# Who copies the transposed queries and keys, and where the first norm transposes stand

## The chip, the cores and the metric

The kernel runs on one NeuronCore of a Trainium2 chip. Its engines work side by side and meet only at semaphores: TensorE (PE in the profile; its weight loads are listed apart as PEld), VectorE (DVE), ScalarE (ACT), GpSimd (POOL) and SyncE (SP), which issues most of the transfers. The metric is the device time of one execution in microseconds, as the median of several runs; lower is better.

## The reference, cut to what matters

There are 16 images of 192 channels and 32 x 32 pixels (1024 tokens). Each passes three layers:

```python
# layer 0: channel attention on a convolved projection
xn = (x - mu) * rsqrt(var + eps) * ln_g + ln_b           # over a whole image
Q, K, V = proj(xn)            # per head of 24 channels: 24 x 24 product, then 3 x 3 depthwise convolution
attn = softmax(einsum("bhnc,bhnd->bhcd", K, Q) / alpha)  # 24 x 24 for each of 8 heads, summed over tokens
x = einsum(V, attn), then w_f, + b_f + xn
# layer 1: causal attention over the 1024 tokens, 6 heads of 32
t = t + attention(ln(t), W_qkv) @ W_proj @ W_proj + ...
# layer 2: 4 experts, each token goes to its best two
t = t + sum over 2 chosen experts of gate * (gelu(ln(t) @ w1 + b1) @ w2 + b2)
```

Layers 0 and 1 are computed image by image. The experts run after the last image, in 67 blocks of 512 rows.

## The kernel before, in words

Each engine has its own program, written out by hand; nothing reorders it. An engine takes its instructions in the written order, and waits stand in it as `wait_ge(semaphore, count)`. What matters here is the part of one image `i` in three stages.

**Stage 1, convolution and channel attention.** PE runs six rounds `conv(i, r)`: four of them ("pair" rounds, p = 0 to 3) give queries and keys of two heads each, two give values. Every round is 32 recorded matmuls of 32 columns by 512 (L1724). ScalarE takes a round out of PSUM with `conv_out` (L1510). For a pair round PE then transposes eight 128 x 128 pieces, `conv_transposes` (L1738): four into PSUM bank 4, four into bank 5. `conv_qk` copies them to the tensor `qkt`: bank 4 on VectorE (L1027, signals `qkT_sb`), bank 5 on ScalarE (L1514, signals `qkT_sb2`). `channel_products(i, f)` (L1751) multiplies keys by queries of two pairs, so it waits for both signals of pairs 2f and 2f + 1; the transposes of pair p wait for the copies of pair p - 1.

Between these copies VectorE does the routing of image `i - 1`, cut into the steps `route(i - 1, 0)` to `route(i - 1, 6)`: gate logits, second layer norm, which two experts a token takes, and the row of each token in its expert's blocks. Step 1 ends with `rowsum` (L1179), the number of tokens per expert; PE's `counts` (L1920, L1921) waits for it and stands between `channel_products(i, 0)` and `conv(i, 4)`. For image 0 the same places hold the steps of `finish_setup`, which prepare weights.

**Stage 2, the tokens.** PE puts together the image's 8 chunks of 128 tokens, one PSUM bank each (`token_bank(k) = k % 6`): `input_and_first_heads(i, k)` (L1772 to L1778) and `last_heads(i, k)` (L1782). VectorE adds a bias to each chunk (L1089, signals `y_sb`), takes its statistics (L1049 to L1056); GpSimd computes the inverse root (L753); VectorE normalises four chunks at a time, `normed(i, 0)` and `normed(i, 1)` (L1065, signals `xhat_sb`). `norm_transposes(i, 0)` on PE (L1791) waits for the first four normalised chunks, which come from token chunks 0 to 3, and writes banks 6 and 7. Chunk 6 reuses the bank of chunk 0 and chunk 7 that of chunk 1, so they wait for `y_sb`.

Then ScalarE copies the transposed tokens (`high_channels`, L1533), VectorE subtracts that copy to get the low part (`low_channels`, L1073 and L1076), and PE makes queries and keys in six groups of five products, `queries_keys` (L1808): the first two products of the first group read the high part, the third waits for L1073, the fourth for L1076. Values (L1816) stand between the groups.

**Stage 3, the softmax attention** of layer 1: 48 units of scores, maxima, exponentials, transposes and products. Its last units hold rounds 0 and 1 of the next image's convolution.

Of the kernel before, what the change touches and what calls it, by code (L numbers as in the profile page):

```python
# [11 lines left out]
ACT = mybir.ActivationFunctionType  # L12
# [3 lines left out]
P = 128  # L16
# [3 lines left out]
def hybrid_block_kernel(nc, x, ln_g, ln_b, conv_w, conv_bias_row, conv_taps, conv_bias, alpha_rows, w_f_t, b_f,  # L20
# [4 lines left out]
    NC = N // P  # L25
# [20 lines left out]
    TPC = BANK // P  # L46
    PAIRS = NH // 2
# [27 lines left out]
    with ExitStack() as ctx:  # L75
# [3 lines left out]
        def at(name, shape, dt, offset):  # L79
            return nc.alloc_sbuf_tensor_at(name, shape, dt, offset=base + offset)  # L80
# [121 lines left out]
        qkt = at("qkt", [P, NC, PAIRS, P], F32, R)  # L202
# [65 lines left out]
        def bank(b, n=1):  # L268
            return ps[:, b * BANK:(b + n) * BANK]
# [4 lines left out]
        def sems(text):  # L274
            return map(sem, text.split())


        conv_ps, qkT_ps, logit_ps, attnT_ps, mix_ps, y_ps = sems("conv_ps qkT_ps logit_ps attnT_ps mix_ps y_ps")
# [4 lines left out]
        chain, qkT_sb, qkT_sb2, lm_sb, attn_sb, attnT_sb, y_sb, veps, xhat_sb, T_lo, qk_lo, mx_sb, PT_dve, linv_sb, at_sb, o_sb = sems(  # L283
            "chain qkT_sb qkT_sb2 lm_sb attn_sb attnT_sb y_sb veps xhat_sb T_lo qk_lo mx_sb PT_dve linv_sb at_sb o_sb")
# [182 lines left out]
        def token_bank(k):  # L467
            return k % 6
# [437 lines left out]
        def _(dve):  # L906
# [116 lines left out]

            def conv_qk(i, p):

                dve.wait_ge(qkT_ps, 2 * (PAIRS * i + p) + 1)
                v.tensor_copy(qkt[:, 0:TPC, p, :], bank(4).rearrange("p (k c) -> p k c", c=P)).then_inc(qkT_sb, 1)  # L1027

# [469 lines left out]
        def _(act):  # L1498
            a = nc.scalar
# [10 lines left out]
                a.activation(dst, bank(2 * (r % 2), 2), ACT.Identity, bias=convb[:, col:col + 1]).then_inc(conv_sb, 1)  # L1510

            def conv_qk(i, p):
                act.wait_ge(qkT_ps, 2 * (PAIRS * i + p) + 2)
                a.activation(qkt[:, TPC:NC, p, :], bank(5).rearrange("p (k c) -> p k c", c=P), ACT.Copy  # L1514
                             ).then_inc(qkT_sb2, 1)
# [170 lines left out]
        def _(pe):  # L1686
# [20 lines left out]
            def conv(i, r):  # L1707
                kind, n = ROUNDS[r]
                if kind == "pair":
                    pe.wait_ge(ring_ld[n], RING_LOADS * (i + 1))  # L1710
                    tiles = [(2 * n + j % 2, W * (j // 2)) for j in range(4)]
                else:
                    tiles = [(HPH * n + j, 2 * W) for j in range(4)]
                if r >= 2:
                    pe.wait_ge(conv_sb, NR * i + r - 1)
                elif i:

                    pe.wait_ge(exp_sb, NU * (i - 1) + NU - 1 + r)
                for nh in range(QC):
                    for s in range(2):  # L1720
                        for j, (h, c0) in enumerate(tiles):
                            rhs = ring[h // 2][s][0:KROWS[s], h % 2, :].rearrange(
                                "p (a b) -> p a b", b=PW)[:, SH // QC * nh:SH // QC * (nh + 1), 0:SW]
                            last = t.matmul(bank(2 * (r % 2) + nh)[W * j:W * (j + 1), :],  # L1724
                                            wconv[s][0:KROWS[s], h, c0:c0 + W], rhs,
                                            start=s == 0, stop=s == 1, skip_group_check=True)
                last.then_inc(conv_ps, 1)
# [28 lines left out]
            def attention_transpose(i, f):  # L1756
                pe.wait_ge(attn_sb, 2 * i + f + 1)
                t.transpose(bank(6 + f)[0:2 * W, P:2 * P], lm[:, f, :], ident[:, :]).then_inc(attnT_ps, 1)
# [10 lines left out]
            def input_and_first_heads(i, k):  # L1769

                o = bank(token_bank(k))
                t.matmul(o[:, 0:HALF], xn[:, 0, P * k:P * (k + 1)], ident[0:HALF, 0:HALF],  # L1772
                         start=True, stop=False, skip_group_check=True)
                t.matmul(o[:, C:CE], xn[:, 0, P * k:P * (k + 1)], gcol[:, :], start=False, stop=False,
                         skip_group_check=True)
                t.matmul(o[:, HALF:CE], xn[:, 1, P * k:P * (k + 1)], ident_g[:, :], start=False, stop=False,
                         skip_group_check=True)
                t.matmul(o[:, 0:CE], vp[:, 0, P * k:P * (k + 1)], mix[:, 0, :], start=False, stop=False,  # L1778
                         skip_group_check=True)

            def last_heads(i, k):
                t.matmul(bank(token_bank(k))[:, 0:CE], vp[:, 1, P * k:P * (k + 1)], mix[:, 1, :], start=False, stop=True,  # L1782
                         skip_group_check=True).then_inc(y_ps, 1)

            def norm_transposes(i, j):
                pe.wait_ge(xhat_sb, NC * i + TPC * (j + 1))
                for b, c0 in ((NORM_BANK[j], 0), (NORM_BANK[j] + 1, P)):
                    if c0:
                        pe.wait_ge(xtwice_sb, 2 * i + j + 1)
                    for kk in range(TPC):  # L1790
                        last = t.transpose(bank(b)[:, P * kk:P * (kk + 1)],  # L1791
                                           xhat[j][:, kk, c0:c0 + P], ident[:, :])
                    last.then_inc(lnT_ps, 1)
# [133 lines left out]
            for i in range(B):  # L1927
                conv(i, 2)
                conv_transposes(i, 1)
                conv(i, 3)  # L1930
                channel_products(i, 0)
                if i:
                    counts(i - 1)
                conv(i, 4)
                conv_transposes(i, 2)
                attention_transpose(i, 0)
                conv(i, 5)
                mixing(i, 0)
                conv_transposes(i, 3)
                pe.wait_ge(mix_sb, 2 * i + 1)  # L1940
                pe.wait_ge(xn_flat, 2 * (i + 1))
                pe.wait_ge(conv_sb, NR * i + 5)
                input_and_first_heads(i, 0)
                channel_products(i, 1)
                input_and_first_heads(i, 1)
                pe.wait_ge(conv_sb, NR * i + 6)
                input_and_first_heads(i, 2)
                attention_transpose(i, 1)
                input_and_first_heads(i, 3)
                mixing(i, 1)  # L1950
                input_and_first_heads(i, 4)
                pe.wait_ge(mix_sb, 2 * i + 2)
                for k in range(4):
                    last_heads(i, k)
                input_and_first_heads(i, 5)
                for k in range(4, 6):
                    last_heads(i, k)
                for k in (6, 7):
                    pe.wait_ge(y_sb, NC * i + k - 5)
                    input_and_first_heads(i, k)  # L1960
                    last_heads(i, k)
                norm_transposes(i, 0)
                for n in range(QK_FIRST):
                    queries_keys(i, n)
                for k in range(2):
                    values_of_tokens(i, k)
                norm_transposes(i, 1)
                for k in range(2, 4):
                    values_of_tokens(i, k)
                for n in range(QK_FIRST, NQ):  # L1970
                    queries_keys(i, n)
                for k in range(4, NC):
                    values_of_tokens(i, k)
                if not i:
                    pe.wait_ge(setup_pool, 8)
                for n in SCORED_FIRST:
                    query_scores(i, n)
                for n, (qc, h) in enumerate(SOFT):
                    for m in SCORED[n]:
                        query_scores(i, m)  # L1980
                    if n == NU - 1 and i + 1 < B:
                        conv(i + 1, 0)
                    blocks(i, n)
                    if i + 1 < B and n in STAT_UNITS:
                        image_stat(i, STAT_UNITS.index(n))
                    if h == 5:
                        four_heads(i, qc)
                    if qc and h == 1:
                        two_heads(i, qc - 1)
                        norms(i, qc - 1)  # L1990
                    if qc and h == 3:
                        output_projection(i, qc - 1)
                if i + 1 < B:
                    conv(i + 1, 1)
                two_heads(i, NC - 1)
                norms(i, NC - 1)
                if i + 1 < B:
                    conv_transposes(i + 1, 0)
                output_projection(i, NC - 1)
# [158 lines left out]
```

## Time and profile before

| what | value |
|---|---|
| median of 3 runs | 3286.74 us (3281.87 to 3288.63) |
| the profiled execution | 3286.35 us |
| its span, first to last instruction | 3284.4 us |
| mean granted TensorE clock, as a share of full speed | 0.988 |
| one image, start of its first channel products to the next one's (image 4 to 5) | 132.2 us |
| busy share of PE, DVE, ACT, POOL | 93%, 67%, 57%, 27% |

The 16 images take the first 2220 us or so of the span, the experts the rest. The images from 1 on repeat each other to within 0.1 us in stages 1 and 2, so one image stands for them all; image 0 (with the setup) and image 15 are different. Image 6 is the one shown. Times in the rows are microseconds from the start of the span.

### The profile page before, as it was taken

Reading aid. Unit: us, or ns where it says so; the run is one execution under the profiler, and the core shown is the slowest. Engines: PE = TensorE matmul, PEld = TensorE weight load, DVE = VectorE, ACT = ScalarE, POOL = GpSimd, SP = SyncE. Lnnn points to the kernel's source line nnn. Section 1 sums busy time; section 2 is a strip of 40 time slices with the busy share of each in tenths; the row PEclk is TensorE's granted clock in tenths of the full one; section 3 lists DMA queues with packets and bytes.
Section 4 is the critical chain, followed back from the end, with each engine's and each line's share of the span. In section 5 each row is a group of like instructions: output and inputs, shape, how many; then the busy total and the mean of one; then the engine's idle time right before and its main releaser. Section 6 shows DMA issues by size and latency. Waiting matters only on the chain.

```text
span 3284.4 us, 72525 instructions
## 1 busy us (share of the span) xinstructions
PE 3069.6 (93%) x26642; PEld 2351.2 (72%) x26642; DVE 2203.7 (67%) x5632; ACT 1870.8 (57%) x3996; POOL 877.6 (27%) x1142
## 2 busy tenths in 40 slices
PE   4999999999999999999999999989999999999995
PEld 1767667666666676766766667668888888888884
DVE  3777677677776777777767877665565555555553
ACT  0548466475574664745647548465555555555553
POOL 2112303313123032131331322352133233233233
PEclk9999999999999999999999999999999999999997
DMA  7446445464464554644545446345676677677673
GB/s 181 133 117 174 127 119 150 122 159 122 125 167 114 142 139 111 180 116 127 150 117 160 121 120 177 100 140 172 187 228 217 203 217 220 202 218 222 199 217 118
DMA packets 256517, 519.83 MB, mean 158 GB/s; under 512 B 70919, under 2 KB 161991, under 8 KB 246521
## 3 DMA queue, kind: packets, MB, share of 16 engines
q1 hardware_dynamic: 222878, 453.58, 49.3%
q0 software_dynamic: 29184, 59.81, 6.1%
q8 instruction: 217, 3.56, 0.5%
q10 hardware_dynamic: 4107, 1.81, 0.3%
q14 instruction: 131, 1.07, 0.1%
HBM read 242.82 MB, written 117.71 MB: 110 GB/s over the span
## 4 chain that ended last, share of the span: by engine, by line
PE 68%; DVE 13%; issue 10%; ACT 3%; POOL 3%; DMA 2%; SPq 1%; DVEq 0%; ACTq 0%; POOLq 0%
PE ps L2048 14%; PE ps L1859 9%; PE ps L2064 9%; PE ps L1847 5%; PE ps L1724 5%; PE ps L2069 5%; PE ps L1808 3%; PE ps L1881 3%; PE ps L1891 2%; PE ps L2024 2%; PE ps L1816 2%; ACT p_sb L1544 2%; DVE minus_max L1095 1%; PE ps L1899 1%; PE ps L2033 1%
## 5 line engine op out<-in xcount | busy, mean ns | idle before, releaser
L1095 DVE TENSOR_REDUCE minus_max<-ps 128x1 f32<-128x128 f32 (+7 forms) x768 | 571.7, 749 | 225.7 <-PE ps L1849 215.2
L1544 ACT ACTIVATE p_sb<-ps,minus_max 128x128 f32<-128x128 f32 (+7 forms) x768 | 570.2, 743 | 42.3 <-DVE minus_max L1095 38.9
L1859 PE MATMUL ps<-ident,p_sb 128*128 128x128 f32 x3456 | 532.8, 279 | 43.5 <-ACT p_sb L1544 15.3
L1429 DVE TENSOR_TENSOR g_lo<-g,g_hi 128x512 fp32r<-128x512 f32 x402 | 281.6, 701 | 362.4 <-ACT g_hi L1670 362.4
L1669 ACT ACTIVATE g<-ps,bcur 128x512 f32<-128x512 f32 x402 | 277.0, 689 | 432.8 <-PE ps L2048 427.5
L1558 ACT ACTIVATE PT<-ps 128x512 f32<-128x512 f32 (+3 forms) x768 | 397.3, 517 | 134.4 <-PE ps L1859 125.4
L1859 PEld LDWEIGHTS ps<-ident,p_sb 128*128 128x128 f32 x3456 | 371.5, 142 | 98.3 <-issue 35.9
L2064 PE MATMUL ps<-w_all,g_hi 128*128 x1608 | 436.5, 352 | 1.7 <-DVE y_rows L1453 1.6
L1847 PE MATMUL ps<-KS,QS 96*128 96x512 f32 (+3 forms) x1152 | 395.0, 402 | 22.6 <-ACT p_sb L1544 19.5
L1724 PE MATMUL ps<-ring,wconv 125*32 125x512 f32 (+1 forms) x3072 | 357.2, 603 | 15.8 <-DMA ring<-padded_scratch 15.8
L817 POOL DMA_INDIRECT routed_rows<-xhat,slot x256 | 254.6, 995 | 349.1 <-issue 346.5
L878 POOL DMA_INDIRECT got<-expert_rows,slot x256 | 258.4, 1009 | 326.1 <-issue 265.4
L765 POOL COPY inverse_wide<-inverse_sums 128x192 f32<-128x192 f32 x128 | 44.2, 346 | 1023.5 <-DVE inverse_sums L1116 1023.5
L2069 PE MATMUL ps<-w_all,g_lo 128*128 x1608 | 292.2, 263 | 0.3 <-DVE g_lo L1429 0.3
L2069 PEld LDWEIGHTS ps<-w_all,g_lo 128*128 128x128 f32 x1608 | 289.3, 188 | 3.0 <-DVE g_lo L1429 1.2
L2064 PEld LDWEIGHTS ps<-w_all,g_hi 128*128 128x128 f32 x1608 | 263.9, 191 | 26.6 <-DVE y_rows L1453 2.4
L1670 ACT ACTIVATE g_hi<-ps,bcur 128x512 fp32r<-128x512 f32 x402 | 273.7, 681 | 0.0
L2048 PE MATMUL ps<-X_hi,cur 128*128 128x512 f32 x780 | 255.6, 409 | 7.1 <-ACT g_hi L1670 4.9
L1847 PEld LDWEIGHTS ps<-KS,QS 96*128 96x128 f32 x1152 | 197.7, 196 | 71.3 <-ACT p_sb L1544 42.8
L2048 PE MATMUL ps<-X,cur 128*128 128x512 f32 x780 | 244.6, 395 | 0.0
L1724 PEld LDWEIGHTS ps<-ring,wconv 125*32 125x32 f32 (+1 forms) x3072 | 93.3, 110 | 207.5 <-issue 193.9
L1108 DVE COPY PT<-ps 128x128 f32<-128x128 f32 (+3 forms) x384 | 184.4, 480 | 68.4 <-PE ps L1859 68.3
(293 smaller groups left out, 5465.6 us busy)
## 6 DMA issues: line engine op xcount, KB each, us to landing
ring<-padded_scratch SPq DMA_DIRECT2D x576, 204.0 KB
cur<-w_all SPq DMA_DIRECT2D x65, 1536.0 KB, 7.1
routed_rows<-zero_rows SPq DMA_DIRECT2D x67, 384.0 KB, 5.1
xgt<-routed_rows SPq DMA_DIRECT2D x67, 384.0 KB, 4.1
expert_rows<-y_rows SPq DMA_DIRECT2D x67, 384.0 KB, 3.3
padded_scratch<-xpad SPq DMA_DIRECT2D x32, 435.0 KB, 3.6
x_sb<-x SPq DMA_DIRECT2D x16, 768.0 KB, 5.5
KS<-QKh SPq DMA_DIRECT2D x128, 96.0 KB
```

The source lines that it names most:

```text
L1095: v.tensor_reduce(nmx[:, qc, h:h + 1], score_place(n), AX, ALU.max, negate=True).then_inc(mx_sb, 1)
L1429: v.tensor_tensor(g_lo[:, n % 2, :], g32[:, n % 2, :], g_hi[:, n % 2, :].bitcast(F32), ALU.subtract).then_inc(lo_sb, 1)
L1544: a.activation(p_sb[n % NP][:, 0:P * (qc + 1)], score_place(n), ACT.Exp, bias=nmx[:, qc, h:h + 1], accum_out=ls[:, qc, h:h + 1]).then_inc( ...
L1558: a.activation(PT[h][:, k0:k0 + nb, :], bank(pass_bank(t))[:, 0:P * nb].rearrange("p (k q) -> p k q", q=P), ACT.Copy).then_inc(PT_act, 1)
L1669: a.activation(g32[:, n % 2, :], bank(n % 2), ACT.Gelu, bias=b1)
L1670: a.activation(g_hi[:, n % 2, :], bank(n % 2), ACT.Gelu, bias=b1).then_inc(gelu_sb, 1)
L1724: last = t.matmul(bank(2 * (r % 2) + nh)[W * j:W * (j + 1), :], wconv[s][0:KROWS[s], h, c0:c0 + W], rhs, start=s == 0, stop=s == 1, skip_g ...
L1847: t.matmul(o[:, k0:k0 + keys], QS[0:96, qc // TPC, h, P * (qc % TPC):P * (qc % TPC + 1)], KS[0:96, h, k0:k0 + keys], start=True, stop=k0 + ...
L1859: last = t.transpose(bank(pass_bank(piece))[:, P * k:P * (k + 1)], p_sb[n % NP][:, P * (k0 + k):P * (k0 + k + 1)], ident[:, :])
L2048: last = t.matmul(bank(n % 2), w[:, W1L * part + P * j:W1L * part + P * (j + 1)], act_part[:, :], start=m == 0, stop=m == 4)
L2064: t.matmul(bank(acc_bank(r, tt))[:, 0:2 * C], g_hi[:, n % 2, P * tt:P * (tt + 1)], w2j, start=j == 0, stop=False, skip_group_check=True)
L2069: last = t.matmul(bank(acc_bank(r, tt))[:, 0:C], g_lo[:, n % 2, P * tt:P * (tt + 1)], w2j[:, 0:C], start=False, stop=j == J - 1, skip_grou ...
```

## The change

Two edits. In the first, `conv_qk` on VectorE returns at once for p = 0, 1 and 2, and ScalarE's `conv_qk` copies bank 4 ahead of bank 5 for those three; the fourth pair keeps its split. In the second, PE's list for stage 2 has `norm_transposes(i, 0)` behind chunk 6 instead of behind chunk 7; the two waits for `y_sb` stay with their chunks.

```diff
@@ VectorE
             def conv_qk(i, p):
 
+                if p != PAIRS - 1:
+                    return
                 dve.wait_ge(qkT_ps, 2 * (PAIRS * i + p) + 1)
                 v.tensor_copy(qkt[:, 0:TPC, p, :], bank(4).rearrange("p (k c) -> p k c", c=P)).then_inc(qkT_sb, 1)
@@ ScalarE
             def conv_qk(i, p):
+                if p != PAIRS - 1:
+                    act.wait_ge(qkT_ps, 2 * (PAIRS * i + p) + 1)
+                    a.activation(qkt[:, 0:TPC, p, :], bank(4).rearrange("p (k c) -> p k c", c=P), ACT.Copy
+                                 ).then_inc(qkT_sb, 1)
                 act.wait_ge(qkT_ps, 2 * (PAIRS * i + p) + 2)
                 a.activation(qkt[:, TPC:NC, p, :], bank(5).rearrange("p (k c) -> p k c", c=P), ACT.Copy
                              ).then_inc(qkT_sb2, 1)
@@ TensorE
-                for k in (6, 7):
-                    pe.wait_ge(y_sb, NC * i + k - 5)
-                    input_and_first_heads(i, k)
-                    last_heads(i, k)
+                pe.wait_ge(y_sb, NC * i + 1)
+                input_and_first_heads(i, 6)
+                last_heads(i, 6)
                 norm_transposes(i, 0)
+                pe.wait_ge(y_sb, NC * i + 2)
+                input_and_first_heads(i, 7)
+                last_heads(i, 7)
```

Line numbers of the kernel after are larger: by 2 on VectorE, by 3 (the new copy itself is L1517) to 6 on ScalarE and PE; L1791 becomes L1797, L1808 becomes L1814.

On PE, the end of stage 2 in image 1, from the last product of chunk 6 to the first products of `queries_keys`. Before:

```order
L1782 MATMUL ps<-mix,vp 128x196
L1772 MATMUL ps<-ident,xn 128x96
L1774 MATMUL ps<-gate_cols,xn 128x4
L1776 MATMUL ps<-ident_gate,xn 128x100
L1778 MATMUL ps<-mix,vp 128x196
L1782 MATMUL ps<-mix,vp 128x196
L1791 MATMUL ps<-ident,xhat_140 128x128 x8
L1808 MATMUL ps<-T_hi,wqkv_a_hi 128x512
```

After:

```order
L1788 MATMUL ps<-mix,vp 128x196
L1797 MATMUL ps<-ident,xhat_140 128x128 x8
L1778 MATMUL ps<-ident,xn 128x96
L1780 MATMUL ps<-gate_cols,xn 128x4
L1782 MATMUL ps<-ident_gate,xn 128x100
L1784 MATMUL ps<-mix,vp 128x196
L1788 MATMUL ps<-mix,vp 128x196
L1814 MATMUL ps<-T_hi,wqkv_a_hi 128x512
```

The five products of chunk 7 have moved from ahead of the eight transposes to behind them; nothing was added.

On VectorE, stage 1 of image 1, from the second normalised chunks of image 0 to its token counts (`xhat_0` is the second layer norm's output, `gx` the exponentials of the gate logits, `chosen` marks the two experts). Before:

```order
L1146 TENSOR_SCALAR xhat_0_142<-t_sb,tmv_106,rstd_107 128x192 x4
L1027 COPY qkt<-ps 128x4x128
L1169 TENSOR_TENSOR gcmp<-gx 128x8x4
L1170 TENSOR_TENSOR geq<-gx 128x8x4
...
L1173 TENSOR_TENSOR geq<-geq,before 128x8x4 x4
L1176 TENSOR_TENSOR gcmp<-gcmp,geq 128x128
L1177 TENSOR_REDUCE gs<-gcmp 128x32
L1178 TENSOR_SCALAR chosen<-gs 128x32
L1179 TENSOR_REDUCE rowsum<-chosen 128x4
```

After:

```order
L1148 TENSOR_SCALAR xhat_0_142<-t_sb,tmv_106,rstd_107 128x192 x4
L1171 TENSOR_TENSOR gcmp<-gx 128x8x4
L1172 TENSOR_TENSOR geq<-gx 128x8x4
...
L1175 TENSOR_TENSOR geq<-geq,before 128x8x4 x4
L1178 TENSOR_TENSOR gcmp<-gcmp,geq 128x128
L1179 TENSOR_REDUCE gs<-gcmp 128x32
L1180 TENSOR_SCALAR chosen<-gs 128x32
L1181 TENSOR_REDUCE rowsum<-chosen 128x4
```

One copy of `qkt` has gone from ahead of the routing; the chain behind it is the same.

On ScalarE, the same stage. Before:

```order
L1566 ACTIVATE norm_sb<-ps 128x256
L1514 ACTIVATE qkt<-ps 128x4x128
L1528 ACTIVATE gx<-gs 128x32
L1510 ACTIVATE vp<-ps,convb 128x1024
L1514 ACTIVATE qkt<-ps 128x4x128
L1510 ACTIVATE qk_pair_159<-ps,convb 128x1024
```

After:

```order
L1572 ACTIVATE norm_sb<-ps 128x256
L1517 ACTIVATE qkt<-ps 128x4x128
L1520 ACTIVATE qkt<-ps 128x4x128
L1534 ACTIVATE gx<-gs 128x32
L1512 ACTIVATE vp<-ps,convb 128x1024
L1517 ACTIVATE qkt<-ps 128x4x128
L1520 ACTIVATE qkt<-ps 128x4x128
L1512 ACTIVATE qk_pair_159<-ps,convb 128x1024
```

A second copy stands ahead of each of the old ones.

## Rows read from the trace of the kernel before

**Rows 1.** The page's busy times, and its chain that ended last.

```profile
PE 3069.6 (93%) x26642; PEld 2351.2 (72%) x26642; DVE 2203.7 (67%) x5632; ACT 1870.8 (57%) x3996; POOL 877.6 (27%) x1142
...
PE 68%; DVE 13%; issue 10%; ACT 3%; POOL 3%; DMA 2%; SPq 1%; DVEq 0%; ACTq 0%; POOLq 0%
```

**Rows 2.** Waits of PE: in total, times, longest us.

```profile
PE ps L1791 <- DVE xhat L1065: 11.3, 15, 2.7
...
PE ps L1920 <- DVE rowsum L1179: 3.3, 15, 0.2
```

**Rows 3.** VectorE's copies of bank 4: duration ns least, median, most.

```profile
L1027 DVE COPY qkt<-ps x64: 681/690/692, 59.4 to 2085.4; 128x512 f32<-128x512 f32 x64
```

**Rows 4.** Timeline of stage 1 in image 6: start, us, what, [idle before <- releaser].

```profile
876.94 0.68 DVE L1027 COPY qkt<-ps 128x512 f32<-128x512 f32 x1
877.03 0.59 ACT L1514 ACTIVATE qkt<-ps 128x512 f32<-128x512 f32 x1
...
878.75 1.15 PE L1751 MATMUL ps<-qkt 128*64 128x64 f32 x32
...
879.87 0.21 DVE L1179 TENSOR_REDUCE rowsum<-chosen 128x4 f32<-128x32 f32 x1
...
880.13 0.38 PE L1920 MATMUL ps<-rowsum,earlier 128*128 128x4 f32 x2 [0.23 <-DVE rowsum L1179]
```

**Rows 5.** Timeline of stage 2 in image 6, chunk 6 to the first products.

```profile
901.50 0.49 PE L1782 MATMUL ps<-mix,vp 128*128 128x196 f32 x2
...
902.41 1.47 DVE L1065 TENSOR_SCALAR xhat<-t_sb,tmv,rstd 128x192 f32<-128x192 f32 x4 [0.58 <-POOL rstd L753]
902.48 0.52 PE L1778 MATMUL ps<-mix,vp 128*128 128x196 f32 x2
...
903.93 1.09 PE L1791 MATMUL ps<-ident,xhat 128*128 128x128 f32 x8 [0.60 <-DVE xhat L1065]
...
905.37 0.47 PE L1808 MATMUL ps<-T_hi,wqkv_a_hi 128*128 128x512 f32 x1 [0.34 <-DVE t_sb L1089]
...
906.42 0.69 DVE L1076 TENSOR_TENSOR T<-ps,T 64x512 fp32r<-64x512 f32 x1
...
907.26 0.47 PE L1808 MATMUL ps<-T,wqkv_b_hi 128*128 128x512 f32 x1 [0.32 <-DVE T L1076]
...
907.57 0.40 PE L1808 MATMUL ps<-T,wqkv_b_lo 128*128 128x512 f32 x1
```

**Rows 6.** Timelines of VectorE and PE in image 0, around its second channel products.

```profile
90.60 0.69 DVE L1027 COPY qkt<-ps 128x512 f32<-128x512 f32 x1
...
91.34 1.98 PE L1751 MATMUL ps<-qkt 128*64 128x64 f32 x32 [2.54 <-DVE qkt L1027]
...
98.72 0.91 PE L1778 MATMUL ps<-mix,vp 128*128 128x196 f32 x2
```

**Rows 7.** Timeline of PE: first work behind four other gaps of 0.99 to 2.74 us.

```profile
985.57 0.42 PE L1891 MATMUL ps<-PT,v_sb 128*32 128x128 f32 x6 [1.53 <-issue]
...
1583.85 0.30 PE L1847 MATMUL ps<-KS,QS 96*128 96x128 f32 x1 [0.99 <-DMA QS<-QKl]
...
2102.57 1.09 PE L1791 MATMUL ps<-ident,xhat 128*128 128x128 f32 x8 [2.74 <-DVE xhat L1065]
...
2185.71 0.66 PE L1859 MATMUL ps<-ident,p_sb 128*128 128x128 f32 x4 [1.35 <-DVE PT L1108]
```

**Rows 8.** Stretches: us, busy us of PE, PEld, DVE, ACT, POOL; granted clock; DMA share, GB/s.

```profile
90.76:104.40 13.64, 13.06 (x75) 11.79 (x76) 6.35 (x12) 0.77 (x3) 0.00 (x0) 0.50 0.15 47
985.57:995.57 10.00, 9.70 (x79) 5.57 (x79) 4.84 (x7) 5.24 (x10) 0.00 (x0) 1.00 0.72 204
1585.80:1592.62 6.82, 6.65 (x40) 4.61 (x38) 3.30 (x10) 5.09 (x23) 4.87 (x5) 0.50 0.91 213
2102.57:2112.57 10.00, 8.97 (x54) 7.17 (x54) 9.11 (x24) 4.57 (x9) 7.52 (x10) 1.00 0.29 86
2186.54:2189.95 3.41, 3.41 (x23) 2.53 (x27) 2.93 (x5) 2.18 (x4) 1.93 (x4) 0.50 0.00 0
```

## The prediction, made before the run

> **What bounds the kernel now.** I read the page's busy times first, then the chain that ended last. PE is busy for 93% of the span and holds 68% of the chain, VectorE only 13% [rows 1]. So time is saved where PE waits, or where VectorE holds PE up, and nowhere else. Next I read PE's waits, because the change touches two places where PE meets VectorE. PE waits 15 times for the token counts `rowsum`, 3.3 us in all and 0.2 each, and 15 times for the normalised chunks `xhat`, 11.3 us in all and 2.7 at most [rows 2]. Last I read the timelines of both places in image 6 [rows 4, 5]. The reader is to see there that the first place is a plain wait of PE, while in the second VectorE works on without a pause and sets the time at which PE goes on.
>
> **Edit 1, three of four copies go to ScalarE.** VectorE loses three copies of 0.69 us an image [rows 3]; ScalarE gets three of 0.59 [rows 4]. What that does to PE is one thing in each image:
>
> - The copy of the second pair stands ahead of the routing (876.94 to 877.62), and `rowsum`, which ends at 880.08, comes some 0.6 us earlier without it. PE waits 0.23 us for `rowsum` ahead of `counts` [rows 4]. A gain of 0.6 covers that whole wait, and PE's own channel products (878.75 for 1.15) are next behind it. 15 images x 0.23 = **-3.45 us**. It can't be more, because no more is waited for there.
> - The other two copies are waited for by nobody: both stand beside a convolution round. They are worth nothing to PE.
> - On ScalarE the danger is that `channel_products(i, 0)` now waits for the second of two copies. Before, that copy ends at 877.62 and the products begin at 878.75, so 1.13 us are free [rows 4]; one more copy of 0.59 leaves 0.54. The cover is the round `conv(i, 3)`, and the price is 0. If it were gone the price would be at most 0.59 x 15 = 8.9 us. The fourth pair, whose products follow at once, keeps its split, so nothing changes there.
> - In image 0 PE waits 2.54 us for VectorE's fourth copy (90.60), which stands behind the setup steps [rows 6]. Of the three copies removed only the third, 0.69 us, lies behind VectorE's last wait for PE, the first channel products. I take **-0.6 us**; the bounds are 0 and all three, -2.1 us.
>
> **Edit 2, the transposes between chunks 6 and 7.** Before, chunk 6 ends at 901.50 + 0.49 = 901.99. Chunk 7 runs until PE falls idle at 903.93 - 0.60 = 903.33, so it is 1.34 us of work. PE then waits 0.60 us for `xhat`, and transposes from 903.93 [rows 5]. `xhat` is VectorE's, 1.47 us from 902.41 and held by GpSimd's root before that; chunk 7 has no part in it. So after the change the transposes still begin at 903.93, and PE is idle from 901.99: one gap of **1.94 us** instead of 0.60.
>
> Behind them: 903.93 + 1.09 for the transposes + 1.34 for chunk 7 = 906.36 for the first product of queries and keys, 0.99 later than its 905.37. Products stand at most 0.31 us apart (907.26 to 907.57), so the fourth would be due at 906.36 + 3 x 0.31 = 907.29. Before, it begins at 907.26, since it waits for VectorE's low part, which ends at 906.42 + 0.69 = 907.11 [rows 5]. The chain `xhat`, transposes, high part, low part is unchanged by the move; chunk 7 only fills PE's small waits inside it. At full clock **edit 2 is worth 0 us**: it moves 1.34 us of work out of one wait of PE into other waits of the same length. VectorE's bias for chunk 7 comes after its low part, at 907.11, and finds the chunk ready, so nothing queues behind it there.
>
> **What the longer gap does to the clock.** This is the term that decides, and no row shows it directly. TensorE's granted clock is either full (2.4 GHz) or half (1.2 GHz), and it falls in this trace around short gaps of PE. Of five gaps that are comparable:
>
> - 2.54 us in image 0 [rows 6]: half clock for 13.64 us
> - 1.53 us at 985.57 [rows 7]: none
> - 0.99 us at 1583.85 [rows 7]: half for 6.82 us
> - 2.74 us at 2102.57, ahead of the same transposes in image 15 [rows 7]: none
> - 1.35 us at 2185.71 [rows 7]: half for 3.41 us; the stretches are [rows 8]
>
> Three of five fell, and the longest did not. The gap of 0.60, which comes in 14 images, was followed by none. So a gap of 1.94 between light products should fall in some images and not in others. I take 8 of 14 (14 x 3/5 = 8.4); the bounds are none and all. In image 15 the gap becomes 2.74 + 1.34 = 4.1 us, longer than any of the five, and I count a fall there: 9 in all.
>
> The price of one: at half clock a product takes 0.91 us instead of 0.52 [rows 6, 5], and PE is dense from here to the end of the stage. A stretch of 3.41 us costs half of it, 1.7 us; one of 6.82 costs 3.4. I take the short one, since the wide products that follow are the densest work of an image. 9 x 1.7 = **+15.3 us**, between 0 and 15 x 3.4 = 51 us.
>
> The Trainium skill, page "TensorE: Matmul & The Clock Gate", section "Why this matters for your kernels", advises against long idle gaps between bursts and names a length for them. By that length no gap of 1.94 us would let the clock fall, the clock term would be nearly 0 and the sum about 3282 us. The trace doesn't bear it out: the gaps of 0.99, 1.35 and 2.54 us above are shorter than the page's and the clock fell by each.
>
> **The sum**, against the profiled execution, 3286.35 us (0.4 below the median of the runs): -3.45 - 0.6 + 0 + 15.3 = +11.2, so **3297.6 us**, 0.3% slower.
>
> **Rivals.**
>
> - *The clock holds (A).* The gap is too short for it, as at 985.57 and 2102.57. Then only the gains count: 3286.35 - 4.05 = 3282.3 us, which is 0.12% and within what can't be told from no change. For it: two of the five gaps. Against it: a chance met 15 times would have to miss each time. The variant in which three or fewer images fall (3 x 1.7 = 5.1) ends at 3287 and belongs here too.
> - *Image 0 is cured (B), the other side.* Its gap shrinks from 2.54 to about 1.9 us, its half-clock stretch of 13.64 us disappears and gives back up to 6.8 us, while the clock holds in the later images: 3282.3 - 6.8 = 3275.5 us, 0.3% faster. It decides from the point where image 0's products run at full clock right behind the gap. For it: the gap is shorter by the third copy. Against it: gaps of 1.35 and 0.99 us did not save the clock elsewhere.
> - *Long stretches (C).* The clock falls in 9 images and stays down for 6.82 us each, as at 1585.8: 3282.3 + 9 x 3.4 = 3313 us. For it: chunk 7, which now stands at the start of the slow stretch, is made of the same small products as image 0's, and those ran slow for 13.64 us. Against it: the queries and keys behind it are wide.
> - *ScalarE is late (D).* Its second copy ends after the products are due. It would take 0.54 us more of delay on ScalarE than the rows show; 3282.3 + 8.9 = 3291 at most without the clock.
>
> **How the numbers follow.** The forecast (falls in four to twelve images, short stretches, 3289 to 3303) gets 0.45, A 0.30, B 0.12, C 0.10, D 0.03. What a measurement of this kernel can tell from no change is about 0.2%, 6.6 us: 3280 to 3293. Slower is C and most of the forecast (those with more than six falls), 0.48; same is A, D and the rest of the forecast, 0.40; faster is B, 0.12. The range leaves out the deepest of B and the longest of C: 3279 to 3307 us.
>
> **What would show each step right or wrong.** The wait of PE for `rowsum` is gone from the waits, and `channel_products(i, 0)` waits for no copy; a wait for ScalarE there would show D. The transposes are preceded by 1.94 us of idle PE in 14 images, and the fourth product of queries and keys begins 3.33 us behind them where the clock held, as it does now (907.26 - 903.93). The granted clock shows stretches of 0.50 at the start of queries and keys in about half of the images, and those images are 1.7 us longer than the rest. The forecast is wrong if there are fewer than four of these, or if `xhat` itself comes earlier, which would turn the gap into a gain.

## The result: 3299.2 us against 3283.1

| kernel | median, us | runs | lowest to highest | ratio to before, 95% interval |
|---|---|---|---|---|
| before | 3283.14 | 6 | 3281.87 to 3288.63 | |
| after | 3299.24 | 6 | 3297.58 to 3305.20 | 1.0044 (1.0032 to 1.0056) |

The changed kernel is 0.4% slower. (The ratios in this document are estimated from the single runs, together with their intervals; they are not the quotients of the medians, which here would be 1.0049.) One run of a kernel of the experiments below, "second copy only", took 4173.71 us at a mean granted clock of 0.655; its ratio leaves that run out, and the median of its other nine is 3281.76 us. The profiled execution of after took 3305.2 us, the longest of its six, with a span of 3302.9; so the two traces differ by 18.5 us where the medians differ by 16.1.

First the busy times, to be held against [rows 1]. PE has the same 26642 matmuls and 9.4 us more of busy time; VectorE has 48 instructions fewer, ScalarE 48 more.

```profile
PE 3079.0 (93%) x26642; PEld 2371.6 (72%) x26642; DVE 2176.8 (66%) x5584; ACT 1893.0 (57%) x4044; POOL 876.0 (27%) x1142
```

The waits of PE, as in [rows 2] (total, times, longest us). The wait for `rowsum` is gone from the list; the wait for `xhat` has grown from 11.3 to 33.9 us.

```profile
PE ps L1797 <- DVE xhat L1067: 33.9, 16, 3.8
```

Stage 1 of image 6 after, against [rows 4]: start, us, what, [idle before <- releaser].

```profile
883.85 0.59 ACT L1517 ACTIVATE qkt<-ps 128x512 f32<-128x512 f32 x1
884.32 0.60 ACT L1520 ACTIVATE qkt<-ps 128x512 f32<-128x512 f32 x1
...
885.57 1.15 PE L1757 MATMUL ps<-qkt 128*64 128x64 f32 x32
...
886.09 0.21 DVE L1181 TENSOR_REDUCE rowsum<-chosen 128x4 f32<-128x32 f32 x1
...
886.65 0.39 PE L1926 MATMUL ps<-rowsum,earlier 128*128 128x4 f32 x2
```

`rowsum` ends at 886.30 and `counts` starts at 886.65, right behind the channel products and 1.08 us after their start; before it was 1.38 (880.13 - 878.75) [rows 4]. ScalarE's second copy ends at 884.92, 0.65 us before the products.

Stage 2 of the same image, where the clock held, against [rows 5]:

```profile
910.45 1.09 PE L1797 MATMUL ps<-ident,xhat 128*128 128x128 f32 x8 [1.94 <-DVE xhat L1067]
911.38 0.36 PE L1778 MATMUL ps<-ident,xn 96*128 96x96 f32 x2
...
912.58 0.53 PE L1814 MATMUL ps<-T_hi,wqkv_a_hi 128*128 128x512 f32 x1
...
913.78 0.47 PE L1814 MATMUL ps<-T,wqkv_b_hi 128*128 128x512 f32 x1 [0.20 <-DVE T L1078]
```

The fourth product begins 913.78 - 910.45 = 3.33 us behind the transposes, as before. And image 2, where it did not hold:

```profile
376.50 1.97 PE L1797 MATMUL ps<-ident,xhat 128*128 128x128 f32 x8 [1.95 <-DVE xhat L1067]
378.26 0.58 PE L1778 MATMUL ps<-ident,xn 96*128 96x96 f32 x2
...
380.59 0.89 PE L1814 MATMUL ps<-T_hi,wqkv_a_hi 128*128 128x512 f32 x1
...
382.13 0.63 PE L1814 MATMUL ps<-T,wqkv_b_hi 128*128 128x512 f32 x1
```

The same eight transposes take 1.97 us instead of 1.09 (in 910.45), and the fourth product comes 5.63 us behind them. The stretches of images 2, 5, 6 and 15 (columns as in [rows 8]; the granted clock is the third number from the end):

```profile
376.36:383.19 6.83, 6.69 (x24) 6.21 (x25) 4.34 (x15) 1.19 (x2) 3.71 (x4) 0.50 0.17 58
...
779.18:782.59 3.41, 3.41 (x10) 2.92 (x10) 2.50 (x8) 0.07 (x2) 2.03 (x3) 0.50 0.17 60
910.45:914.45 4.00, 3.79 (x24) 3.26 (x25) 3.83 (x12) 1.08 (x2) 2.79 (x3) 1.00 0.23 80
2117.22:2124.05 6.83, 5.62 (x21) 5.35 (x22) 5.26 (x18) 1.19 (x2) 3.70 (x4) 0.50 0.17 58
```

Going through all images this way, a stretch at half clock begins around the start of the first norm transposes in 9 of the 14 images from 1 to 14 (1, 2, 4, 5, 8, 9, 11, 13, 14), and in image 0; in image 15 one begins in the wait ahead of them, which is 3.79 us long there. In the trace of before there was none at this place in any image.

### The profile page after: what moved, and what is told of

The parts are those of the page before. It is cut to its first block, busy times and chain, and to the rows that moved or that the text cites. A ratio compares the mean times of both kernels' runs of the same rounds, so it can differ in the third digit from the quotient of the medians.

```text
span 3302.9 us, 72524 instructions
## 1 busy us (share of the span) xinstructions
PE 3079.0 (93%) x26642; PEld 2371.6 (72%) x26642; DVE 2176.8 (66%) x5584; ACT 1893.0 (57%) x4044; POOL 876.0 (27%) x1142
## 3 DMA queue, kind: packets, MB, share of 16 engines
q10 hardware_dynamic: 4107, 1.81, 0.3%
## 4 chain that ended last, share of the span: by engine, by line
PE 76%; DVE 9%; issue 6%; ACT 3%; DMA 2%; POOL 2%; SPq 1%; DVEq 0%; ACTq 0%; POOLq 0%
PE ps L2056 13%; PE ps L1730 10%; PE ps L1865 9%; PE ps L2072 9%; PE ps L1853 5%; PE ps L2077 5%; PE ps L1887 3%; PE ps L1814 3%; PE ps L1897 2%; PE ps L2032 2%; ACT p_sb L1550 2%; PE ps L1822 2%; PE ps L1905 2%; DVE minus_max L1097 1%; PE ps L1744 1%
```

## Experiments

The theory: edit 1 is a small gain; edit 2 costs nothing by itself, and loses time only through the clock, which falls at the longer gap. The rivals: the copies on ScalarE are what costs, or the new order costs even at full clock. All eight kernels below were timed beside the kernel before; the first four share 29 of its runs (median 3283.97 us), the last four 23 (3286.73 us).

| kernel | median, us | ratio to before, 95% interval | idle PE ahead of the transposes, images 1 to 14 | falls there | stage 1, us |
|---|---|---|---|---|---|
| before | | | 0.60 | 0 of 14 | 18.75 |
| after | 3299.24 | 1.0044 (1.0032 to 1.0056) | 1.94 | 9 of 14 | 18.45 |
| copies only | 3280.12 | 0.9989 (0.9978 to 1.0) | 0.60 | 0 | 18.46 |
| order only | 3300.86 | 1.0052 (1.0039 to 1.0065) | 1.94 | 12 | 18.74 |
| gap filled | 3276.14 | 0.9977 (0.9968 to 0.9985) | 0.41 | 0 | 18.46 |
| last product only | 3278.38 | 0.9983 (0.9972 to 0.9994) | 0.94 | 0 | 18.45 |
| gap half filled | 3280.03 | 0.9978 (0.9968 to 0.9988) | 1.18 | 0 | 18.45 |
| second copy only | 3282.31 | 0.9984 (0.997 to 0.9997) | 0.60 | 0 | 18.45 |
| table later | 3274.74 | 0.9959 (0.9944 to 0.9974) | 0.60 | 0 | 18.45 |
| gap filled, table later | 3269.01 | 0.9948 (0.9931 to 0.9965) | 0.41 | 0 | 18.46 |

Stage 1 is counted from the first channel products of an image to its first `last_heads` product. A fall is a stretch at half clock that begins within 1 us ahead of the first norm transposes of an image or 3.5 us behind their start. The idle times, falls and stage lengths are of the one profiled execution of each kernel, the medians of all its runs. Between the two groups of runs the kernel before itself moved by 2.8 us, so kernels of different groups are best compared by their ratios.

### Edit 1 alone

```diff
                 conv_qk on VectorE and ScalarE as in after
-                input_and_first_heads(i, 6); last_heads(i, 6)
-                norm_transposes(i, 0)
-                input_and_first_heads(i, 7); last_heads(i, 7)
+                input_and_first_heads(i, 6); last_heads(i, 6)
+                input_and_first_heads(i, 7); last_heads(i, 7)
+                norm_transposes(i, 0)
```

> Edit 1 alone: ScalarE copies both halves for the first three pairs, PE's order as before. My theory (the loss is the clock behind the longer gap ahead of the transposes, edit 1 is a small gain): in images 1 to 14 stage 1 is 0.30 us shorter, the gap ahead of the transposes is 0.60 us, no stretch at half clock begins there, and the time is 4 to 8 us under before, 3275 to 3280 us. Rival (ScalarE, with 48 more copies, is what costs): the time stays 10 us or more above before, and PE waits for a copy of ScalarE in stage 1.

Measured: 3280.12 us, just above the expected range; stage 1 is shorter by 0.29 to 0.30 us in each image from 1 to 15, and the old gap is back. Waits of PE in this kernel (the line for `rowsum` is absent):

```profile
PE ps L1797 <- DVE xhat L1067: 12.5, 16, 2.5
```

The copies are no loss: this kernel is 19.1 us below after, whose only difference is the order. Whether they are a gain for the median is just at the edge of what the runs tell (the interval ends at 1.0); the timeline shows 15 x 0.30 = 4.5 us.

### Edit 2 alone

```diff
                 conv_qk on VectorE and ScalarE as in before
+                norm_transposes(i, 0) between chunks 6 and 7, as in after
```

> Edit 2 alone: the copies as before, the first norm transposes between chunks 6 and 7. My theory: 1.94 us of idle PE ahead of the transposes, half clock behind it in 7 to 11 of images 1 to 14 and in image 15, 1.2 to 2.8 us lost for each, so 17 to 23 us above before, 3300 to 3306 us. Rival (the copies cost): within 4 us of before.

Measured: 3300.86 us, 0.5% above before and at the low end of what was expected. PE still waits for `rowsum`, and the transposes of image 3 show the clock:

```profile
PE ps L1791 <- DVE xhat L1065: 34.2, 16, 4.1
...
PE ps L1920 <- DVE rowsum L1179: 3.2, 15, 0.2
```

```profile
506.94 1.97 PE L1791 MATMUL ps<-ident,xhat 128*128 128x128 f32 x8 [1.94 <-DVE xhat L1065]
```

```profile
506.90:513.73 6.83, 6.79 (x24) 6.31 (x25) 4.25 (x14) 1.26 (x3) 3.77 (x4) 0.50 0.17 58
```

Twelve of 14 images fell (all but 2 and 10), ten of them for 3.41 us and two for 6.83. The whole loss is in the order; that the copies cost is refuted by both kernels.

### The gap filled

```diff
                 last_heads(i, 6)
+                for n in range(14):
+                    t.transpose(bank(NORM_BANK[0] + n % 2)[:, 0:P], ident[:, :], ident[:, :])
                 norm_transposes(i, 0)
```

> The kernel after, with 14 transposes of the identity matrix in the gap ahead of the first norm transposes, into banks 6 and 7, whose contents the norm transposes overwrite; they compute nothing that is used. They take about 1.6 of the 1.94 us, so PE waits some 0.3 us. My theory (the gap lowers the clock, the order itself costs nothing): no stretch at half clock begins at the transposes, the fourth product of queries and keys starts 3.33 us behind the first transpose in every image from 1 to 14, and the time is that of edit 1 alone, 3275 to 3281 us, although PE has 224 more instructions. Rival (the order costs by itself, because chunk 7 pushes queries and keys back): no change against the kernel after, 3297 to 3303 us.

Measured: 3276.14 us, 23.1 below after, with 224 instructions more on PE. The timeline of PE in image 2, and the stretch from its transposes to the fourth product:

```profile
368.41 1.69 PE L1968 MATMUL ps<-ident 128*128 128x128 f32 x14
370.51 1.09 PE L1797 MATMUL ps<-ident,xhat 128*128 128x128 f32 x8 [0.41 <-DVE xhat L1067]
...
372.64 0.53 PE L1814 MATMUL ps<-T_hi,wqkv_a_hi 128*128 128x512 f32 x1
...
373.84 0.47 PE L1814 MATMUL ps<-T,wqkv_b_hi 128*128 128x512 f32 x1 [0.20 <-DVE T L1078]
```

```profile
370.51:373.84 3.33, 3.12 (x21) 2.67 (x22) 3.20 (x10) 1.08 (x2) 2.72 (x3) 1.00 0.26 89
```

This decides between the theory and the rival of the order. The order of after is unchanged, chunk 7 stands behind the transposes as there, and the fourth product comes 3.33 us behind them in all 14 images. Only PE's idleness is gone, and with it the loss. The order by itself costs nothing that these runs can tell; the loss comes with the idle time and the half clock around it.

### Only the last product of chunk 7 behind the transposes

```diff
+                input_and_first_heads(i, 7)
                 norm_transposes(i, 0)
-                input_and_first_heads(i, 7)
                 last_heads(i, 7)
```

> The kernel after, but of chunk 7 only the last product (two recorded matmuls, 0.33 us) stands behind the transposes. The gap is then 0.60 + 0.33 = about 0.93 us. My theory, with a fall that depends on how long the gap is: no fall or at most 3 in images 1 to 14, 3275 to 3283 us. Rival (any transposes ahead of the end of chunk 7 cost the same): 3297 us or more.

Measured: 3278.38 us, no fall in images 1 to 14. PE in image 2:

```profile
373.17 1.09 PE L1797 MATMUL ps<-ident,xhat 128*128 128x128 f32 x8 [0.94 <-DVE xhat L1067]
374.10 0.50 PE L1788 MATMUL ps<-mix,vp 128*128 128x196 f32 x2
```

### The gap half filled

```diff
-                for n in range(14):
+                for n in range(7):
```

> The kernel after with 7 instead of 14 transposes of the identity matrix in the gap, so PE still waits some 1.1 to 1.2 us ahead of the norm transposes (0.41 with 14, 1.94 with none). My theory, a fall that depends on how much PE idles there: none or few of images 1 to 14 fall, since neither 0.93 us with one product moved nor 0.41 us did; 3274 to 3283 us. Rival (any idle time over 1 us makes the clock fall at the rate of after, 9 of 14): 3285 us or more.

Measured: 3280.03 us, no fall in images 1 to 14, with 1.18 us of idle PE:

```profile
367.94 0.93 PE L1968 MATMUL ps<-ident 128*128 128x128 f32 x7
370.05 1.09 PE L1797 MATMUL ps<-ident,xhat 128*128 128x128 f32 x8 [1.18 <-DVE xhat L1067]
```

At this place the loss is therefore not spread evenly over the length of the gap: idle times of 0.41, 0.60, 0.94 and 1.18 us gave no fall in any image from 1 to 14, and 1.94 us gave 9 and 12. Lengths between 1.18 and 1.94 were not tried in these images, but image 0 has some at the same place: with 1.40 us the clock fell in neither of two kernels (gap filled, with and without the later table), with 1.60 us in two of three (second copy only and table later, not copies only), and with 1.94 us and more in all four.

### Only the second pair's copy moved

```diff
-                if p != PAIRS - 1:
+                if p == 1:
```

> Of edit 1 only the copy of the second pair, the one ahead of the routing, goes to ScalarE; the first and third stay on VectorE, PE's order as before. My theory: this copy alone gives the whole 0.30 us an image in stage 1 (18.45 us from the first channel products to the first last_heads product, as with all three), because only rowsum was waited for. Rival (the other two count too): the stage is between 18.5 and 18.75 us.

Measured: 3282.31 us, and stage 1 takes 18.45 us, as with all three. So the copy ahead of the routing carries the whole gain of stage 1, and the other two carry none in images 1 to 15.

### The table of the first blocks later, with and without the filled gap

In image 15 PE idles 2.25 to 4.07 us ahead of these transposes in every kernel above, the filled one too (2.25), because VectorE does the 13 steps of `front_table` there. The two kernels spread them over the softmax of that image; one has PE's order of before, the other the filled gap.

```diff
                     block_table(i)
-                    if i == B - 2:
-                        front_table()
@@ the softmax units of the last image
+                    if i + 1 == B and n == 2:
+                        table_steps = front_table()
+                    if i + 1 == B and 4 <= n < 4 + 13:
+                        next(table_steps, None)
```

> Edit 1 alone, and the 13 steps of front_table, which VectorE does at the end of stage 1 of image 15, spread over softmax units 4 to 16 of that image. The page's rows show 2.4 to 2.7 us of idle PE ahead of image 15's transposes behind it, and a later start of the stage. I expect the transposes of image 15 at 6.43 us behind its first last_heads product instead of 9.5, no wait over 0.7 us there, and 3 us less than edit 1 alone (3277 us against 3280), if the 13 steps find VectorE free in units 4 to 16. Rival: they delay the maxima there and give it back.

> The kernel after with the gap filled by 14 transposes of the identity matrix (they compute nothing that is used), and front_table spread over the softmax of image 15. If both gains are real and independent: 3 us less than with the filled gap alone, 3273 us, the fastest of all. If the filling only replaces clock falls that chance makes anyway, the same as the later table alone, 3277 us.

Measured: 3274.74 us for the first, 5.4 below edit 1 alone (0.9959 of before against 0.9989), where 3 were expected; the trace accounts for the 3 at the transposes and not for the rest. Image 15's transposes now stand 6.43 us behind its first `last_heads` product like every other image's, and its softmax stage (from its first scores to PE's first work for the experts) takes 85.67 us, against 85.80 with edit 1 alone, so nothing was given back:

```profile
2092.35 1.09 PE L1809 MATMUL ps<-ident,xhat 128*128 128x128 f32 x8 [0.60 <-DVE xhat L1067]
```

For the second 3269.01 us, 0.52% below before and the lowest median of this study; 4 us less than expected. It is below the filled gap alone (0.9948 with an interval to 0.9965, against 0.9977 from 0.9968), though its 14 extra transposes an image compute nothing and only keep the clock up. Against the later table alone (0.9959) the intervals overlap, and so do those of the filled gap (0.9977) and of edit 1 alone (0.9989); that filling the gap gains over the order of before is therefore not shown. No image from 1 to 14 falls at this place in any of the four. The profiled executions differ elsewhere: with edit 1 alone the clock fell once inside a softmax stage (for 6.83 us from 521.3, image 3, whose stage took 93.98 us instead of 91.9) and once in stage 2 of image 15 (for 6.83 us from 2094.8, a stage of 27.02 us), and in neither place with the gap filled (24.68 us there), but that is one execution of each.

## Why the prediction was right, point by point

| term | forecast, us | measured in the profiled executions, us |
|---|---|---|
| stage 1, images 1 to 15 | -3.45 | 15 x -0.30 = -4.5 |
| image 0 | -0.6 | -3.8, not shown to be the edit's (see below) |
| new order at full clock | 0 | 0: 3.33 us to the fourth product where the clock held |
| falls in images 1 to 14 | 8 x 1.7 = 13.6 | 9, +16.9 in stage 2 |
| image 15 | 1.7 | +1.9 |
| not forecast: softmax stages | 0 | +6.2 |
| not forecast: start of image 0's channel products | 0 | +2.4 |
| not forecast: from the experts on | 0 | -0.5 |
| sum | +11.2 | +18.6 (the spans differ by 18.5) |

The forecast of 3297.6 us lies 1.6 from the measured median, but part of that is luck: it was counted from an execution 3.2 us above the median that before has over six runs, so the change itself, +11.2, was forecast 4.9 short of the +16.1 of the medians. The places and the mechanism of the loss were right; the falls, the softmax stages and image 0 were off by 3 to 6 us each, with opposite signs.

**Edit 1.** Right in place and mechanism: the wait for `rowsum` is gone, ScalarE was in time with 0.65 us left (0.54 was forecast), and one copy of the three makes the gain. The size was short by 0.07 us an image. I took the wait of the matmul, 0.23 us [rows 4], as the most there was to gain; the channel products could have been followed at 1.08 us instead of 1.38, because the weight load ahead of `counts` waited longer than the matmul, as this row of before shows:

```profile
880.13 0.30 PEld L1920 LDWEIGHTS ps<-rowsum,earlier 128*128 128x128 f32 x2 [0.37 <-DVE rowsum L1179]
```

**Image 0.** The term of -0.6 rests on a wait that did not repeat. In the profiled execution of after it went from 2.54 to 1.61 us, and the stretch of 13.64 us at half clock, which I had left to rival B, did not occur:

```profile
93.26 1.15 PE L1757 MATMUL ps<-qkt 128*64 128x64 f32 x32 [1.61 <-DVE qkt L1029]
```

```profile
93.20:99.00 5.80, 5.74 (x68) 5.10 (x69) 3.13 (x8) 0.77 (x3) 0.00 (x0) 1.00 0.45 127
```

So the first half of rival B came true in these two traces and its second half, a clock that holds in the later images, did not. But the edit isn't shown to be the cause. With edit 2 alone, where the copies are those of before, the same wait is short too and the products behind it run at full clock:

```profile
92.51 1.15 PE L1751 MATMUL ps<-qkt 128*64 128x64 f32 x32 [0.29 <-DVE qkt L1027]
```

Stage 1 of image 0 took 28.32 us before and between 22.67 and 26.57 in the nine other kernels, 24.48 in this one. The wait of 2.54 us and the long stretch stand in the trace of before alone, and what made them is open.

**Edit 2 at full clock.** The step "PE is idle from 901.99, one gap of 1.94 us" came to the hundredth (1.94 in image 6, 33.9 us over 16 images), and so did its worth of 0. The filled gap shows this without the clock's share.

**The clock.** The deciding step, three of five comparable gaps and so 8 of 14 images, was met by 9 here and 12 with edit 2 alone. The agreement is partly luck: the five gaps it came from lie in other places and between other work, and one of 0.99 us was counted as a fall although 1.18 us at this place never gave one. Nor were they all: the trace of before has gaps of 0.94 and 0.93 us at 2096.90 and 2201.96, with no fall, and of 1.41 and 1.51 us at 2205.41 and 2207.57, with one fall around them. The price was mis-sized from one side: five of the nine stretches lasted 6.83 us and cost 2.7 us each (image 2: 24.29 us from the first `last_heads` product to the first scores, against 21.56), four lasted 3.41 us and cost 1.2. The mean is 2.0 where 1.7 was forecast. (Nine such falls make 18.3 us; stage 2 of images 1 to 14 grew by 16.9, mainly because image 11 took 22.70 us before already, with the wait of 0.99 us for a transfer ahead of its first scores [rows 7].) Both kinds are cheaper than half their length, since PE has small waits for VectorE there that the slower products fill: the fourth product of queries and keys stands 0.60 us behind the third at full clock (image 6), and 0.43 at half clock (image 5: 781.02 and 781.45).

**The rule of the Trainium skill** (page "TensorE: Matmul & The Clock Gate", section "Why this matters for your kernels"), by whose length no gap of 1.94 us would lower the clock, is not borne out at this place: the clock fell behind 9 and behind 12 of 14 such gaps.

**Image 15.** Its +1.9 us came near the 1.7, but the trace doesn't tie it to edit 2: with edit 1 alone and the old order, after a wait of 2.45 us, the clock fell there too, and stage 2 took 27.02 us against 26.81 in after and 24.91 before.

**What stays open.** The softmax stages were 6.2 us longer in sum in the profiled execution of after. They differ between executions of all kernels (1464 to 1475 us in sum). In after four of them hold a wait of PE of 1.25 to 1.81 us that the profile gives no releaser for (images 1, 6, 9 and 11; before has one, of 1.53), and in image 6 the clock also fell for 6.83 us from 929.4:

```profile
PE ps L1897 <- issue: 6.4, 4, 1.8
```

No experiment was made on them. The medians of after and of edit 1 alone differ by 19.1 us, and stage 2 of images 1 to 14 by 17.8 in their profiled executions, so they are not needed for the verdict.

## What to carry to other kernels

Before a step is moved ahead into a wait, ask what was filling the time until that wait ended: here 1.34 us of products were moved out of a stretch in which PE had nothing else, to a place where they were hidden anyway, and what changed was how long PE stood still at a stretch. In this kernel idle time of TensorE that cost nothing at full clock was not free, because the granted clock fell around it and the dense work that follows ran at half speed; read the clock of the stretch behind each new gap, and price it by the next stage's work at half speed. Where such a gap can't be avoided, products that compute nothing are worth a try: here they were cheaper than the gap.

## What the runs showed of the hardware

- Ahead of the first norm transposes of images 1 to 14, with the same work on both sides, idle times of 0.41, about 0.60, 0.94 and 1.18 us never lowered the clock (112 gaps in eight kernels, 84 of them of about 0.60 us or less), and 1.94 us lowered it in 21 of 28.
- The chance of a fall also grew with the length at a second place, the softmax stages of images 1 to 14, where PE has 13 waits of over 1.2 us without a releaser in the ten profiled kernels: of six of them, from 1.25 to under 1.8 us, none had a fall at it or close behind, of four of 1.80 or 1.81 us two had, of three from 2.09 to 2.35 us all three.
- The length alone doesn't decide. Ahead of the same transposes in image 15, 2.25, 2.74 and 3.02 us lowered it in none of three kernels, and 2.45 us (in two kernels) and 2.78 us did. And a wait of 1.33 to 1.35 us near the end of image 15's softmax stage (that of 2185.71 in [rows 7]) stands in all ten kernels and was followed by a fall in six.
- A gap of 1.94 us lowers the clock in some images and not in others of the same program, and for 3.41 or for 6.83 us.
- The 14 transposes of the identity that filled the gap took 1.69 us an image, and with them the median fell from 3299.24 to 3276.14 us.
